# Four fused layers on one core: GpSimd makes both parts of W_hh, eight banks for columns, late products of 128 rows

## The chip, the core and the metric

The kernel runs on one core of one Trainium2 chip. Its engines are TensorE (PE, matrix products; PEld is its weight load), VectorE (DVE), ScalarE (ACT), GpSimd (POOL) and SyncE (SP, which here only issues transfers). Each runs its own list of instructions in order, and they wait for each other by semaphores. The metric is the device time of one execution in microseconds, as a median of several.

## What is computed

Four layers, each added to its input; `x` is 4 batches of 512 rows of 512 values in fp32.

```python
x = x + L0(fside, cond, x)      # a 0/1 mask of the 5120 largest entries of an outer product times softmax(x), per batch
x = x + L1(x, cond, W_emb, b_emb, g_norm, W_qkv, g_q, g_k, W_out)
    # xn = rms_norm(x) * g_norm * (1 + scale) + shift;  q, k, v = split(xn @ W_qkv), 16 heads of 32
    # q, k = rms_norm per head; o = softmax(q @ k.T / sqrt(32)) @ v;  returns o + o @ W_out
x = x + L2(cond, x, W_ih, W_hh, b_ih, b_hh)
    # a GRU over 512 steps: gi = x_t @ W_ih + b_ih, gh = h @ W_hh + b_hh, gates r, z, n, new h
x = x + L3(x, cond)             # each row sampled at 512 places given by cond, with linear interpolation
```

## The kernel before

It has one hand-written program for each engine (`pe_program`, `dve_program`, `act_program`, `pool_program`, `sp_program`); the order of the lines is the order of the work, and semaphores named in `SEMAPHORES` tie them. There are eight PSUM banks of 128 x 512 fp32, reached as `k.bank(i, ...)`.

First comes a search for the mask's threshold for all four batches. Then the attention of the batches runs one after another, `b` from 0 to 3. A batch has these stages:

- Columns (`pe_columns`, `act_columns`, `dve_columns`): PE transposes `x` (L1610) into banks 0 and 1, which DVE copies to `xT` (L1201), and multiplies it by a diagonal of the row norms (L1617) into banks 2 and 3, which ACT scales to `xnT` (L692). Four column groups `c`, two at a time, use the same four banks twice.
- Projection (`pe_project`, L1640) of four row tiles `t` to q, k and v, three outputs of 4 products each. For each tile ACT takes squares and copies (L704, L705), DVE sums, normalizes (L1230), and ACT and DVE split the heads to a high and a low fp16 part (L719, L1244), which PE transposes (`pe_turn_stack`, L1659) and ACT and DVE copy out (L728, L1252). POOL scales the keys between (`pool_keys`, L494). Beside this lie, for the next batch, the mask (`dve_mask_equal`, `dve_mask_prefix`, `dve_mask_quota`, `dve_mask_taken` on DVE, `pool_mask` on POOL) and the row powers (L675 on ACT); for the previous batch the output products (`pe_out_matmuls`, L1682), with POOL's L517 and DVE's L1261 that add to `xT`.
- The attention loop over 32 units, 8 for each of four head groups `g`. In a unit PE makes two score products (L1703), DVE their maxima (L1272), somebody negates them (L509 on POOL in batches 0 to 2, L1275 on DVE in batch 3), ACT takes exponentials (L743), PE transposes them (L1719), ACT and DVE copy the transposes (L788, L1351), and PE multiplies by the values (L1737). After each group DVE inverts the sums (L1359), POOL spreads them (L465), PE turns them (L1752, the divide), ACT copies (L750) and DVE multiplies (L1283, which counts `out_cols`).

In batch 3 there is no next batch. Instead DVE finds the scale of W_hh (`dve_hh_scale`), ACT writes the scaled fp16 high part `w_kept` (`act_high_weights`, L665), DVE the remainder in place (`dve_low_weights`, L1101), and POOL copies the high part behind it (`pool_keep_weights`, L485): chunks 0 and 1 after tile 1, chunks 2 and 3 after tile 2, as `WEIGHT_CHUNKS` says.

After the last batch's output products, PE makes the first gate products (L1814), and then the recurrence starts (`pe_gru`): 512 steps of 96 small products each (L1907). `SIDE` puts other products between the steps: gate products of later chunks (L1814) and the sampling of finished rows, 128 rows by 256 columns (L1841). The rows 384 to 447 are sampled from step 464 on by `pe_late_products` (L1854), with 64 rows in 4 products, two records each, at one product a step over 32 steps; rows 448 to 479 follow from step 496, the last 32 at the end.

Of the kernel before, what the change touches and what calls it, by code (L numbers as in the profile page):

```python
# [16 lines left out]
P = 128  # L17
B, S, D = 4, 512, 512
NT = S // P
# [53 lines left out]
prepared sums absmax hh_most hh_scale w_high w_low w_kept  # L73
# [299 lines left out]

R_BANK, Z_BANK, N_BANK, SIDE_BANK = (0, 3), (1, 4), (2, 5), (6, 7)


def sp_program(e, k):
# [43 lines left out]
def pool_program(e, k):  # L421
# [21 lines left out]
    for b in range(B):  # L443
# [27 lines left out]
WEIGHT_CHUNKS = ((), (0, 1), (2, 3), ())  # L471


# [8 lines left out]
def pool_keep_weights(e, k, c):  # L482
    s = k.sem
    e.wait_ge(s["w_low"], c + 1)
# [176 lines left out]
def act_high_weights(e, k, c):  # L661
    s = k.sem
    if c == 0:
        e.wait_ge(s["hh_scale"], 5)
    e.activation(k.w_kept[:, c], k.w_hh_raw[:, c], ACT.Copy, scale=k.hh[2][:]).then_inc(s["w_high"], 1)  # L665


# [16 lines left out]
def act_columns(e, k, b):  # L684
# [5 lines left out]
    for c in range(NC):  # L690
        e.wait_ge(s["normed_turned"], NC * b + c + 1)
        e.activation(k.xnT[:, c], k.bank(2 + c % 2, S), ACT.Identity, scale=k.col_scale[:, c, b:b + 1],  # L692
# [60 lines left out]
def act_attention(e, k, b, logit_scale):  # L753
    s = k.sem
    act_take_projected(e, k, b, 0)
    for t in range(1, NT):
# [6 lines left out]
        if b == B - 1:  # L763
            for c in WEIGHT_CHUNKS[t]:
                act_high_weights(e, k, c)
        elif t == 1:
            act_row_powers(e, k, b + 1)
        elif t == 2:
# [67 lines left out]
def act_take_late_rows(e, k, i, bank):  # L836
    s = k.sem
    b, part = divmod(i, ROW_GROUPS)
    rows = slice(0, LATE[1] - LATE[0])
# [258 lines left out]
def dve_low_weights(e, k, c):  # L1098
    s = k.sem
    e.wait_ge(s["w_high"], c + 1)  # L1100
    e.scalar_tensor_tensor(k.w16[:, c, 0].rearrange("p a n -> p (a n)"), k.w_hh_raw[:, c], k.hh[2][:], k.w_kept[:, c],  # L1101
                           ALU.mult, ALU.subtract).then_inc(s["w_low"], 1)


# [84 lines left out]
def dve_columns(e, k, b):  # L1189
# [9 lines left out]
    for c in range(NC):  # L1199
        e.wait_ge(s["x_turned"], NC * b + c + 1)  # L1200
        e.tensor_copy(k.xT[:, c, b], k.bank(c % 2, S)).then_inc(s["x_cols"], 1)  # L1201
# [98 lines left out]
def dve_attention(e, k, b):  # L1300
    s = k.sem
    if b + 1 < B:
        dve_mask_equal(e, k, b + 1)
        dve_mask_prefix(e, k, b + 1)
        dve_mask_quota(e, k, b + 1)
        dve_mask_taken(e, k, b + 1)
    else:
        dve_hh_scale(e, k)
    dve_take_projected(e, k, b, 0)
    for t in range(1, NT):  # L1310
# [3 lines left out]
        dve_stack(e, k, b, t - 1, 0)  # L1314
        dve_turn_stack(e, k, b, t - 1, 0)
        dve_stack(e, k, b, t - 1, 1)
        dve_take_projected(e, k, b, t)
        if b == B - 1:
            for c in WEIGHT_CHUNKS[t]:
                dve_low_weights(e, k, c)  # L1320
        elif t == 2:
# [276 lines left out]
def pe_columns(e, k, b):  # L1598
# [4 lines left out]
    for first in range(0, NC, 2):  # L1603
        for c in (first, first + 1):
            if c >= 2:
                e.wait_ge(s["x_cols"], NC * b + c - 1)
            elif b:
                e.wait_ge(s["exp"], 2 * len(UNITS) * b)
            for t in range(NT):
                made = e.transpose(k.bank(c % 2, S)[:, t * P:(t + 1) * P], k.x[:, b, t, c * P:(c + 1) * P], k.ident[:])  # L1610
            made.then_inc(s["x_turned"], 1)
        for c in (first, first + 1):
            e.wait_ge(s["diagonals"], NT * (b + 1))
            if c >= 2:
                e.wait_ge(s["x_normed"], NC * b + c - 1)
            for t in range(NT):
                made = e.matmul(k.bank(2 + c % 2, S)[:, t * P:(t + 1) * P], k.x[:, b, t, c * P:(c + 1) * P], k.diagonal[b][:, t],  # L1617
# [336 lines left out]
```

## Time and profile before

| | us |
|---|---|
| median of 3 runs | 2307.71 |
| lowest, highest | 2306.45, 2307.78 |
| profiled execution, its own time | 2310.08 |
| its span in the trace | 2308.4 |
| mean granted TensorE clock | 0.968 |
| PE busy | 2181.9 (95%) |
| DVE busy | 1558.8 (68%) |
| ACT busy | 1276.3 (55%) |
| POOL busy | 501.5 (22%) |

Busy time is an average over stages with different limits. The chain of work that ended last is followed backwards from the last instruction to what released each step, and tells where time could be won. Starts in the rows are microseconds from the start of the span; durations of PE are modelled at their ends, so that starts are the better measure of a pace.

### The profile page before, as it was taken

To read this page: it belongs to the slowest core of one execution; us is meant where nothing else is said; L and a number is where in the kernel's file an instruction comes from. 1 tells how busy PE (TensorE), PEld (TensorE's weight loads), DVE (VectorE), ACT (ScalarE), POOL (GpSimd) and SP (SyncE) were. 2 spreads that over 40 slices of the span, in tenths; PEclk is the share of its full clock that TensorE was granted. 3 is DMA by queue.
4 is the path that set the end of the run, shared out by engine and by line. 5 is a ranking of instruction groups with operands and counts; after the bars stand their busy time and mean duration, and the time that the engine had idled before them with its cause. 6 is when DMAs were issued, how large, how long until landed. Compare 5 with 4: busy or idle time off the path is not lost.

```text
span 2308.4 us, 132456 instructions
## 1 busy us (share of the span) xinstructions
PE 2181.9 (95%) x56333; PEld 1833.7 (79%) x56333; DVE 1558.8 (68%) x7118; ACT 1276.3 (55%) x5574; POOL 501.5 (22%) x2261
## 2 busy tenths in 40 slices
PE   5768999999989999999999999999999999999998
PEld 3654555645545799999999999999999999999887
DVE  7986867768678366666676666666666667666665
ACT  6755947758558344566444444544445444444443
POOL 2001121021110222233222222222222222222222
PEclk8568999999999999999999999999999999999999
DMA  5000000010010000000000000000000000000000
GB/s 202 3 2 1 1 1 1 2 55 1 1 55 1 21 5 5 5 5 5 5 5 10 5 10 5 10 10 5 10 9 5 9 5 10 10 5 14 12 9 16
DMA packets 8728, 31.63 MB, mean 14 GB/s; under 512 B 1028, under 2 KB 1352, under 8 KB 7880
## 3 DMA queue, kind: packets, MB, share of 16 engines
q1 hardware_dynamic: 7712, 23.07, 2.7%
q8 instruction: 444, 7.27, 1.3%
q14 instruction: 148, 1.21, 0.2%
q10 hardware_dynamic: 424, 0.07, 0.0%
HBM read 18.94 MB, written 4.19 MB: 10 GB/s over the span
## 4 chain that ended last, share of the span: by engine, by line
PE 84%; DVE 10%; ACT 3%; issue 2%; DMA 1%; POOL 0%; SPq 0%; DVEq 0%; POOLq 0%; ACTq 0%
PE psum L1907 52%; PE psum L1814 9%; PE psum L1640 5%; PE psum L1719 4%; PE psum L1737 3%; PE psum L1703 2%; PE psum L1682 2%; PE psum L1841 2%; DVE region_cols L1095 2%; DVE region_cols L1079 2%; DVE top L1272 1%; PE psum L1659 1%; DMA region_cols<-in_L_cond_W_emb_dram 1%; PE psum L1854 1%; PE psum L1752 1%
## 5 line engine op out<-in xcount | busy, mean ns | idle before, releaser
L1907 PE MATMUL psum<-parts0A,region_w_hh 128*128 128x40 f16 x12288 | 431.4, 182 | 3.4 <-DVE parts0A L1496 2.3
L1907 PE MATMUL psum<-parts1A,region_w_hh 128*128 128x40 f16 x12288 | 428.7, 181 | 2.9 <-DVE parts1A L1496 2.6
L1907 PE MATMUL psum<-parts0B,region_w_hh 128*128 128x40 f16 x12288 | 427.7, 181 | 0.4 <-issue 0.2
L1907 PE MATMUL psum<-parts1B,region_w_hh 128*128 128x40 f16 x12288 | 426.4, 181 | 0.6 <-issue 0.5
L1907 PEld LDWEIGHTS psum<-parts0A,region_w_hh 128*128 128x128 f16 x12288 | 381.0, 96 | 44.6 <-DVE parts0A L1496 11.5
L1907 PEld LDWEIGHTS psum<-parts1A,region_w_hh 128*128 128x128 f16 x12288 | 377.6, 96 | 44.9 <-DVE parts1A L1496 13.2
L908 ACT ACTIVATE mixA<-rzA 128x8 f32<-128x8 f32 x512 | 111.3, 217 | 541.9 <-DVE rzA L1451 541.9
L1907 PEld LDWEIGHTS psum<-parts0B,region_w_hh 128*128 128x128 f16 x12288 | 363.1, 96 | 1.6 <-issue 0.2
L1907 PEld LDWEIGHTS psum<-parts1B,region_w_hh 128*128 128x128 f16 x12288 | 361.4, 96 | 2.1 <-issue 0.8
L551 POOL TENSOR_SCALAR lineA<-lineA 128x8 f32<-128x8 f32 x511 | 121.7, 238 | 853.8 <-DVE lineA L1487 853.8
L1451 DVE TENSOR_REDUCE rzA<-psum 128x8 f32<-128x32 f32 x512 | 98.1, 192 | 255.6 <-PE psum L1907 254.3
L1814 PE MATMUL psum<-region_cols,region_w_a 128*128 128x256 f32 (+1 forms) x864 | 252.5, 389 | 0.9 <-DVE region_cols L1261 0.9
L743 ACT ACTIVATE region_rows<-psum,neg_top 128x512 f32<-128x512 f32 x256 | 173.9, 686 | 34.5 <-POOL neg_top L509 23.2
L551 POOL TENSOR_SCALAR lineB<-lineB 128x8 f32<-128x8 f32 x511 | 125.3, 245 | 287.4 <-DVE lineB L1487 287.4
L1272 DVE TENSOR_REDUCE top<-psum 128x2 f32<-128x1024 f32 x128 | 156.2, 1222 | 38.4 <-PE psum L1703 38.3
L915 ACT ACTIVATE giveB<-rzB 128x8 f32<-128x8 f32 x512 | 109.0, 213 | 131.4 <-DVE rzB L1458 131.0
L1640 PE MATMUL psum<-region_w_a,region_work 128*128 128x512 f32 x384 | 173.5, 605 | 3.5 <-ACT region_work L692 3.5
L1719 PEld LDWEIGHTS psum<-ident,region_rows 128*128 128x128 f32 x1024 | 118.5, 141 | 34.8 <-issue 18.7
L1466 DVE TENSOR_TENSOR_SCAN nlineA<-mixA,psum 128x32 f32<-128x32 f32 x512 | 113.0, 221 | 43.2 <-ACT mixA L908 0.7
L1719 PE MATMUL psum<-ident,region_rows 128*128 128x128 f32 x1024 | 136.2, 275 | 4.8 <-ACT region_work L788 4.1
L1640 PEld LDWEIGHTS psum<-region_w_a,region_work 128*128 128x128 f32 x384 | 72.2, 193 | 86.0 <-issue 81.7
L922 ACT ACTIVATE lineA<-nlineA 128x8 f32<-128x8 f32 x512 | 111.6, 218 | 47.4 <-DVE nlineA L1466 1.0
(245 smaller groups left out, 3709.1 us busy)
## 6 DMA issues: line engine op xcount, KB each, us to landing
region_rows<-in_x_dram SPq DMA_DIRECT2D x4, 1024.0 KB, 11.2
region_w_a<-in_L_cond_W_qkv_dram SPq DMA_DIRECT2D x1, 3072.0 KB, 23.1
region_w_hh<-in_L_cond_W_hh_dram SPq DMA_DIRECT2D x4, 768.0 KB, 6.4
region_w_a<-in_L_cond_W_ih_dram SPq DMA_DIRECT2D x1, 3072.0 KB, 10.3
out_dram<-region_w_b SPq DMA_DIRECT2D x12, 256.0 KB, 2.6
region_cond<-in_cond_dram SPq DMA_DIRECT2D x2, 1024.0 KB, 7.8
region_cols<-in_L_cond_W_emb_dram SPq DMA_DIRECT2D x1, 2048.0 KB, 19.7
region_w_out<-in_L_cond_W_out_dram SPq DMA_DIRECT2D x1, 1024.0 KB, 21.5
```

The lines of the kernel that those rows point to most:

```text
L551: e.tensor_scalar(k.line[half][:, :, :, 1], k.line[half][:, :, :, 2], -1.0, None, ALU.mult).then_inc(s[f"minus{h}"], 1)
L743: e.activation(k.probs[b][:, 2 * pair + i], k.bank(2 * pair + i, S), ACT.Exp, scale=logit_scale, bias=k.neg_top[:, col + i:col + i + 1], a ...
L908: e.activation(k.mix[half][:, :, :, 3], k.rz[half][:, 0], ACT.Sigmoid, scale=unscale).then_inc(s[f"rsig{h}"], 1)
L915: e.activation(k.give[half][:, :, :, 2], k.rz[half][:, 1], ACT.Sigmoid, scale=minus_unscale).then_inc(s[f"give{h}"], 1)
L922: e.activation(k.line[half][:, :, :, 0], k.nline[half][:, :, :, 3], ACT.Tanh, scale=unscale).then_inc(s[f"tanh{h}"], 1)
L1272: e.tensor_reduce(k.top[:, cols], k.psum[:, 2 * pair:2 * pair + 2], AX.X, ALU.max).then_inc(s["top"], 1)
L1451: e.tensor_reduce(k.rz[half][:, 0], k.slots(R_BANK[half])[:, 0], AX.X, ALU.add).then_inc(s[f"rsum{h}"], 1)
L1466: e.tensor_tensor_scan(k.nline[half][:].rearrange("p c b q -> p (c b q)"), k.mix[half][:].rearrange("p c b q -> p (c b q)"), k.bank(N_BANK ...
L1640: made = e.matmul(k.bank(bank, D), k.xnT[:, c, t * P:(t + 1) * P], k.w_qkv[:, c, i * D:(i + 1) * D], start=(c == 0), stop=(c == NC - 1))
L1719: made = e.transpose(k.bank(bank, NT, P)[:, kt], k.probs[b][:, slot, kt * P:(kt + 1) * P], k.ident[:])
L1814: made = e.matmul(k.bank(SIDE_BANK[number % 2], B * LENGTHS[q]), k.w_ih[:, c, block * P:(block + 1) * P], k.xT[:, c, :, STARTS[q]:STARTS[q ...
L1907: made = e.matmul(k.slots(bank)[:, :, ch, :, 0:2], k.w16[:, 2 * read + c, part, NC * "rzn".index(g) + 2 * half + ch], k.parts[now][read][: ...
```

## The change

Five edits. (1) `act_high_weights` and `dve_low_weights` are gone; a new `pool_split_weights` does all of it on POOL, one chunk before each wait for `inv_weight` in batch 3: a scaled copy to `w_kept`, a scaling of the raw chunk in place, their difference to the low part, the copy of the high part. (2) The columns stage has a bank for each of the eight products, with the order: two transposed groups, four normed groups, two transposed groups. The first projection waits for two of the four copies to `xT`, the second for all. (3) In batch 0 DVE's `dve_mask_quota` moves behind the taking of the first projection and `dve_mask_taken` behind the first stack. (4) The last batch's output products `m` = 0 and 1 first take three of four groups `c`, then the fourth, and then come `m` = 2 and 3. (5) The late products take 128 rows, 320 to 447, as weights; the 64 wanted ones are then in partitions 64 to 127, from where they are copied and written out.

```diff
+TURNED_BANK, NORMED_BANK = (0, 1, 4, 5), (2, 3, 6, 7)
@@ sp_program
-        e.dma_start(k.d_out[b, LATE[0]:LATE[1]], k.rows_out[0:LATE[1] - LATE[0], b]).then_inc(s[f"out{b}"], 16)
+        e.dma_start(k.d_out[b, LATE[0]:LATE[1]], k.rows_out[P - (LATE[1] - LATE[0]):, b]).then_inc(s[f"out{b}"], 16)
@@ pool_program
-            if t and b == B - 1:
-                for c in WEIGHT_CHUNKS[t]:
-                    pool_keep_weights(e, k, c)
         for g in range(NC):
+            if b == B - 1:
+                pool_split_weights(e, k, g)
@@
+def pool_split_weights(e, k, c):
+    s = k.sem
+    low = k.w16[:, c, 0].rearrange("p a n -> p (a n)")
+    if c == 0:
+        e.wait_ge(s["hh_scale"], 5)
+    e.tensor_scalar(k.w_kept[:, c], k.w_hh_raw[:, c], k.hh[2][:], None, ALU.mult).then_inc(s["w_high"], 1)
+    e.tensor_scalar(k.w_hh_raw[:, c], k.w_hh_raw[:, c], k.hh[2][:], None, ALU.mult).then_inc(s["w_scaled"], 1)
+    e.wait_ge(s["w_high"], c + 1)
+    e.wait_ge(s["w_scaled"], c + 1)
+    e.tensor_tensor(low, k.w_hh_raw[:, c], k.w_kept[:, c], ALU.subtract).then_inc(s["w_low"], 1)
     e.wait_ge(s["w_low"], c + 1)
     e.tensor_copy(k.w16[:, c, 1].rearrange("p a n -> p (a n)"), k.w_kept[:, c]).then_inc(s["w_kept"], 1)
@@ act_attention
-        if b == B - 1:
-            for c in WEIGHT_CHUNKS[t]:
-                act_high_weights(e, k, c)
@@ dve_attention
-        dve_mask_quota(e, k, b + 1)
-        dve_mask_taken(e, k, b + 1)
+        if b:
+            dve_mask_quota(e, k, b + 1)
+            dve_mask_taken(e, k, b + 1)
     dve_take_projected(e, k, b, 0)
+    if b == 0:
+        dve_mask_quota(e, k, b + 1)
     for t in range(1, NT):
         dve_norm_heads(e, k, b, t - 1)
         dve_stack(e, k, b, t - 1, 0)
+        if b == 0 and t == 1:
+            dve_mask_taken(e, k, b + 1)
...
-        if b == B - 1:
-            for c in WEIGHT_CHUNKS[t]:
-                dve_low_weights(e, k, c)
@@ pe_columns
+    for c in (0, 1):
+        pe_turn_rows(e, k, b, c)
+    for c in range(NC):
+        pe_norm_rows(e, k, b, c)
+    for c in (2, 3):
+        pe_turn_rows(e, k, b, c)
+def pe_turn_rows(e, k, b, c):
+    if b and c == 0:
+        e.wait_ge(s["exp"], 2 * len(UNITS) * b)
+    elif b and c >= 2:
+        e.wait_ge(s[("probs_act", "probs_dve")[c - 2]], len(UNITS) * b)
...
+def pe_norm_rows(e, k, b, c):
+    if b and c >= 2:
+        e.wait_ge(s[("out_cols", "inv_cols")[c - 2]], NC * b)
...
@@ pe_project
         if t == 0:
-            e.wait_ge(s["x_cols"], NC * (b + 1))
+            e.wait_ge(s["x_cols"], NC * b + 2)
         elif t == 1:
+            e.wait_ge(s["x_cols"], NC * (b + 1))
@@ pe_out_matmuls
-    e.wait_ge(s["out_cols"], NC * (b + 1))
+    e.wait_ge(s["out_cols"], NC * b + cs[-1] + 1)
@@ pe_attention
-        pe_out_matmuls(e, k, b, range(NC))
+        pe_out_matmuls(e, k, b, (0, 1), range(NC - 1))
+        pe_out_matmuls(e, k, b, (0, 1), range(NC - 1, NC))
+        pe_out_matmuls(e, k, b, (2, 3))
@@ pe_late_products
-        made = e.matmul(k.bank(SIDE_BANK[number % 2], HALF_ROW)[0:LATE[1] - LATE[0]], k.xT[:, c, b, LATE[0]:LATE[1]],
+        made = e.matmul(k.bank(SIDE_BANK[number % 2], HALF_ROW), k.xT[:, c, b, LATE[1] - P:LATE[1]],
```

## Rows read from the trace of the kernel before

**Rows 1.** The page: the chain that ended last, by engine.

```profile
PE 84%; DVE 10%; ACT 3%; issue 2%; DMA 1%; POOL 0%; SPq 0%; DVEq 0%; POOLq 0%; ACTq 0%
```

**Rows 2.** Stages of batches 2, 3: window, length, busy us (PE, PEld, DVE, ACT, POOL), clock.

```profile
455.77:515.83 60.06, 58.26 (x223) 28.34 (x224) 42.68 (x68) 28.50 (x46) 16.23 (x12) 1.00 0.14 53
604.27:671.52 67.25, 60.30 (x219) 29.36 (x220) 45.33 (x59) 31.48 (x41) 18.72 (x13) 0.95 0.13 47
```

**Rows 3.** Timeline of ACT, DVE and PE in batch 3: start, us, instruction, idle before.

```profile
631.15 3.02 ACT L665 ACTIVATE region_rows<-region_w_hh,hh_scale 128x1536 f16<-128x1536 f32 x2
...
632.75 3.55 DVE L1101 SCALAR_TENSOR_TENSOR region_w_hh<-region_w_hh,hh_scale,region_rows 128x1536 f16<-128x1536 f32 x2 [1.11 <-ACT region_rows L665]
...
641.84 1.89 PE L1659 MATMUL psum<-ident,region_work 128*128 128x128 f16 x16 [4.51 <-DVE region_work L1244]
...
659.15 1.07 PE L1659 MATMUL psum<-ident,region_work 128*128 128x128 f16 x16 [2.44 <-DVE region_work L1244]
```

**Rows 4.** POOL's groups by form: busy us, mean ns, idle before; then one timeline row.

```profile
L551 POOL TENSOR_SCALAR lineA<-lineA 128x8 f32<-128x8 f32 x511 | 121.7, 238 | 853.8 <-DVE lineA L1487 853.8
...
L558 POOL COPY region_work<-lineA 128x8 f32<-128x8 f32 x512 | 97.7, 191 | 1.6 <-DVE lineA L1487 1.6
...
L494 POOL TENSOR_TENSOR region_work<-region_work,gain 128x512 f32<-128x512 f32 x16 | 20.3, 1270 | 308.4 <-DVE region_work L1230 308.4
...
L465 POOL COPY region_cond<-inv_weight 128x512 f32<-128x512 f32 x16 | 9.8, 610 | 97.6 <-DVE inv_weight L1359 97.6
...
715.05 0.61 POOL L465 COPY region_cond<-inv_weight 128x512 f32<-128x512 f32 x1 [17.66 <-DVE inv_weight L1359]
```

**Rows 5.** DVE's L1244 beside POOL (timeline), and spreads of single durations in ns.

```profile
639.15 2.63 DVE L1244 TENSOR_TENSOR region_work<-region_work 128x512 f16<-128x512 f32 x2 [1.12 <-ACT region_work L719]
...
639.32 3.79 POOL L485 COPY region_w_hh<-region_rows 128x1536 f16<-128x1536 f16 x2
...
L1244 DVE TENSOR_TENSOR region_work<-region_work x32: 677/772/1943, 180.8 to 669.3; 128x512 f16<-128x512 f32 x32
...
L1275 DVE TENSOR_TENSOR neg_top<-top,minus_logit_scale x32: 160/161/163, 677.8 to 746.7; 128x2 f32<-128x2 f32 x32
```

**Rows 6.** Batch 3's loop, DVE's timeline.

```profile
710.10 0.16 DVE L1275 TENSOR_TENSOR neg_top<-top,minus_logit_scale 128x2 f32<-128x2 f32 x1
...
712.09 0.16 DVE L1275 TENSOR_TENSOR neg_top<-top,minus_logit_scale 128x2 f32<-128x2 f32 x1
...
714.90 1.16 DVE L1272 TENSOR_REDUCE top<-psum 128x2 f32<-128x1024 f32 x1
```

**Rows 7.** Columns of batch 3 on PE; DVE's `quota` in batch 1.

```profile
597.92 1.04 PE L1610 MATMUL psum<-ident,region_rows 128*128 128x128 f32 x8
...
598.79 1.95 PE L1617 MATMUL psum<-region_rows 128*128 128x128 f32 x16
...
604.27 20.87 PE L1640 MATMUL psum<-region_w_a,region_work 128*128 128x512 f32 x48 [0.87 <-ACT region_work L692]
...
318.24 0.16 DVE L1163 TENSOR_SCALAR quota<-psum 128x4 f32<-128x4 f32 x1 [2.18 <-PE psum L1595]
```

**Rows 8.** Batch 0, PE's first stack transposes.

```profile
183.27 1.06 PE L1659 MATMUL psum<-ident,region_work 128*128 128x128 f16 x16
```

**Rows 9.** The chain at the last divide and the output products.

```profile
752.80 1.10 PE psum L1752 x8
...
755.38 14.02 PE psum L1682 x32
```

**Rows 10.** PE's timeline: starts of steps with row products, then with late products.

```profile
2127.86 0.97 PE L1907 MATMUL psum<-parts0A,region_w_hh 128*128 128x40 f16 x32
...
2130.80 0.96 PE L1907 MATMUL psum<-parts1A,region_w_hh 128*128 128x40 f16 x32
...
2154.40 0.97 PE L1907 MATMUL psum<-parts1A,region_w_hh 128*128 128x40 f16 x32
...
2160.57 0.60 PE L1907 MATMUL psum<-parts1A,region_w_hh 128*128 128x40 f16 x17
```

More of the change, by code:

```diff
@@ L72 @@
 const vec emb_products emb_rows row_max weighted exp_rows diagonal keys_act keys_dve
-prepared sums absmax hh_most hh_scale w_high w_low w_kept
+prepared sums absmax hh_most hh_scale w_high w_scaled w_low w_kept
 mask_made mask_summed sum_copied counted ranked signed bound highs lows
@@ L658, in act_bound @@
     e.activation(k.bound[:, col], old, ACT.Identity, scale=2.0, bias=k.way[:, col]).then_inc(s["bound"], 1)
[L661 to L665, printed above, removed]
 def act_row_powers(e, k, b):
@@ L691, in act_columns @@
         e.wait_ge(s["normed_turned"], NC * b + c + 1)
-        e.activation(k.xnT[:, c], k.bank(2 + c % 2, S), ACT.Identity, scale=k.col_scale[:, c, b:b + 1],
+        e.activation(k.xnT[:, c], k.bank(NORMED_BANK[c], S), ACT.Identity, scale=k.col_scale[:, c, b:b + 1],
                      bias=k.col_shift[:, c, b:b + 1]).then_inc(s["x_normed"], 1)
@@ L762, in act_attention @@
         act_take_projected(e, k, b, t)
-        if b == B - 1:
-            for c in WEIGHT_CHUNKS[t]:
-                act_high_weights(e, k, c)
-        elif t == 1:
+        if b + 1 < B and t == 1:
             act_row_powers(e, k, b + 1)
-        elif t == 2:
+        elif b + 1 < B and t == 2:
             act_row_roots(e, k, b + 1)
@@ L838, in act_take_late_rows @@
     b, part = divmod(i, ROW_GROUPS)
-    rows = slice(0, LATE[1] - LATE[0])
+    rows = slice(P - (LATE[1] - LATE[0]), P)
     e.wait_ge(s["rows_sum"], TILE_ROWS + i + 1)
@@ L1095, in dve_mask @@
         e.tensor_scalar(mask, k.lows[:, b], 2.0 ** -(LOW_BITS - 1 - i), k.bound[:, col], ALU.mult, ALU.is_ge).then_inc(s["mask_made"], 1)
[L1098 to L1102, printed above, removed]
 def dve_mask_equal(e, k, b):
@@ L1200, in dve_columns @@
         e.wait_ge(s["x_turned"], NC * b + c + 1)
-        e.tensor_copy(k.xT[:, c, b], k.bank(c % 2, S)).then_inc(s["x_cols"], 1)
+        e.tensor_copy(k.xT[:, c, b], k.bank(TURNED_BANK[c], S)).then_inc(s["x_cols"], 1)
 def dve_take_projected(e, k, b, t):
@@ L1317, in dve_attention @@
         dve_take_projected(e, k, b, t)
-        if b == B - 1:
-            for c in WEIGHT_CHUNKS[t]:
-                dve_low_weights(e, k, c)
-        elif t == 2:
+        if b + 1 < B and t == 2:
             dve_row_scales(e, k, b + 1)
@@ L1602, in pe_columns @@
         e.wait_ge(s["bound"], B * (HIGH_BITS + LOW_BITS))
[L1603 to L1617, printed above, removed]
-                                start=True, stop=True)
-            made.then_inc(s["normed_turned"], 1)
+    for c in (0, 1):
[10 more added lines that the diff above has]
+        e.wait_ge(s[("probs_act", "probs_dve")[c - 2]], len(UNITS) * b)
+    for t in range(NT):
+        made = e.transpose(k.bank(TURNED_BANK[c], S)[:, t * P:(t + 1) * P], k.x[:, b, t, c * P:(c + 1) * P], k.ident[:])
+    made.then_inc(s["x_turned"], 1)
+def pe_norm_rows(e, k, b, c):
+    s = k.sem
+    if c == 0:
+        e.wait_ge(s["diagonals"], NT * (b + 1))
+    if b and c >= 2:
+        e.wait_ge(s[("out_cols", "inv_cols")[c - 2]], NC * b)
+    for t in range(NT):
+        made = e.matmul(k.bank(NORMED_BANK[c], S)[:, t * P:(t + 1) * P], k.x[:, b, t, c * P:(c + 1) * P], k.diagonal[b][:, t],
+                        start=True, stop=True)
+    made.then_inc(s["normed_turned"], 1)
 def pe_project(e, k, b, t, outputs):
```

2 lines of the change are left out of this document (removed).

## The prediction

> **What bounds the kernel now.** I read the page first. The chain that ended last is 84% TensorE (PE) [rows 1]. So PE's own work or what PE waits for is worth time; VectorE (DVE), ScalarE (ACT) and GpSimd (POOL) count only where PE stands. Next I cut the span by the chain into the search, four attention batches, the output products of the last one (755.38 to 769.40) [rows 9] and the recurrence. The stage table then compares like with like: from the first projection to the third output product, batch 2 takes 60.06 us with PE busy 58.26, batch 3 67.25 with PE busy 60.30 at a mean granted clock of 0.95 of its upper level, 2.4 GHz [rows 2]. Batch 3 has two holes, 4.51 and 2.44 us, both ended by DVE's L1244; before each, ACT's L665 and DVE's L1101 work on W_hh [rows 3]. The lower clock, seen in this window and not in batch 2's, comes with the first hole.
>
> **W_hh leaves ACT and DVE.** Four L665 and four L1101 go. Two pairs of 3.02 and 3.55 us [rows 3] overlap only in part, so up to 5 us of delay lies ahead of each L1244. Without them PE is next late at its own pace: batch 2 shows 58.3 us of work for the same stage, and batch 3 has no L675 on ACT. That would give 67.25 - 58.3 = 9.0 us.
>
> **W_hh goes to POOL.** A chunk is now a scaled copy to fp16, a scaling in place, a subtraction and the known copy L485, two of which take 3.79 us [rows 5], each over 1536 columns. The trace has no long POOL TENSOR_SCALAR. With 8 columns it takes 238 ns where a copy takes 191 [rows 4], so I take the copy's 1.9 us; the lower end is 1.5, from L465 (610 ns for 512 fp32), the upper the price of a two-input operation. That one is L494 or L517 at 1.27 us for 512, less some 0.15 of fixed cost three times over: 3.5 us. A chunk is 1.9 + 1.9 + 3.5 + 1.9 = 9.2 us, at most 12.4. POOL stands idle 17.66 us before each spread L465 [rows 4], so the spread, and PE's divide behind it, are not late. Nor is the start of the recurrence, which waits for `w_low` and `w_kept`: chunk 3 starts near 734 and ends before 750.
>
> **What that cover hides badly.** DVE and POOL hold each other up. At 639.15 two L1244, some 1.3 us by the least single time (677 ns, the ends overlapping), took 2.63: its second, due at about 639.8, ran only when POOL's copy (639.32 + 1.90) had ended [rows 5]. One L1244 took 1943 ns against a median of 772 [rows 5]. I read it as: a DVE operation with both inputs in SBUF waits for the whole POOL operation under way, then goes ahead of the next. In batch 3's loop that is L1275, the negated maximum, once per unit of 1.98 us; behind it on DVE is queued the copy L1351 that PE's next transposes wait for, and ACT's exponentials (L743) wait for L1275 itself. L1275 never met POOL (160 to 163 ns), so the bounds are nothing and full blocking; I take full blocking, because L1244 has the same kind of operation and of inputs. The page "SBUF — State Buffer" of the Trainium skill, section Who interferes with whom, says the same of a DVE instruction with two SBUF inputs beside a GpSimd instruction that reads SBUF, and calls one with at most one SBUF input free outside the two-port modes. By that rule the loop loses the 8.7 us worked out next; if it does not reach an operation on two columns, the loop loses nothing and 8.7 us come back.
>
> In the loop DVE runs reduce, L1275, copy; none of the rows names an idle time before them, 710.10 to 712.09 being one unit [rows 6]. A chunk starts at about 715.7, after the spread (715.05 + 0.61) [rows 4]. The next L1275 comes at 716.06, the end of the reduce begun at 714.90, and waits to 717.6: 1.5 us. Another comes 1.9 us after it, when the in-place scaling is just over: 0. The next meets the subtraction: 3.5 - 1.9 = 1.6. The last copy costs 0 again. That is 3.1 us a chunk, 2.9 with what slack PE has, and chunks 1 to 3 cost 3 x 2.9 = 8.7. Chunk 0 starts at the end of L494 of the last tile, just when the last four L1244 want to run (the last of one kind starts at 669.3) [rows 5]. Each lets one POOL operation pass; the fourth ends behind the subtraction, some 5 us after PE could use it. Of the 9.0 us, 9.0 - 5.1 = 3.9 are left. Net of all W_hh edits: 3.9 - 8.7 = -4.8, a loss.
>
> **Eight banks for columns, and the first batch's order.** Now PE runs transposes and normed products in two rounds and ACT finishes after the last, from 597.92 to 604.27: 6.35 us [rows 7]. Of this PE stands the last 0.87 for ACT's L692. Two groups of transposes take 0.87 by the starts (597.92 to 598.79). In the new order PE does just these while ACT finishes, so the stage is 6.35 - 0.87 = 5.5, a gain of 0.9. DVE gets its last two columns about 1.6 us later, so its mask or scale work starts later. In batches 1 and 2 it stood 2.18 us before `quota` (row at 318.24) [rows 7], which covers it but for some 0.3: gain 0.6 each. In batch 3 DVE is done before PE's first stack transposes: 0.9. In batch 0 the same step gives 1.1, PE's slow first products at the start of the stage unchanged. There the delay would eat DVE's margin, but `quota` and `taken` move behind the first projection's taking and the first stack, and a wait such as batch 1's is filled; PE reaches its first stack transposes at 183.27 with no idle either way [rows 8]. POOL's mask and ACT's L675 behind `taken` keep their place. New waits on banks 4 to 7 are for things done long before. Sum 1.1 + 0.6 + 0.6 + 0.9 = 3.2.
>
> **Output products of the last batch.** PE stands from the end of the divide, 752.80 + 1.10 = 753.90, to 755.38 for ACT's L750 and DVE's L1283 [rows 9]. Six of the 16 products (14.02 x 6/16 = 5.3 us) now fill this. The end moves by 1.5. The last addition still comes behind m = 3, and POOL's four L517 (at about 1.3 each, as L494) stay ahead of the additions.
>
> **Late products.** Two of the 32 late steps take 2160.57 - 2154.40 = 6.17 us, 3.085 each; a step with L1841, the same moving shape but 128 x 128 weights, takes 2.94 (2127.86 to 2130.80) [rows 10]. So the bigger load hides, and the 64-column form does not. 32 x 0.145 = 4.6. Lower end 0, if the reason is not the shape. The eight copies out of partitions 64 to 127 cost what they did.
>
> **Sum.** -4.8 + 3.2 + 1.5 + 4.6 = 4.5 us. The profiled execution took 2310.08 with a span of 2308.4 and would take 2305.6; its execution lies 2.4 above the median 2307.71, so the median comes to 2303.2. I write 2303.
>
> **Rivals.** (1) L1275 is not held up, or only for what is left of a short piece. For it: no small DVE operation of the recurrence is ever long beside POOL's. Against: L1244. Then 8.7 come back, and perhaps 3 before the loop: 2303 - 8.7 to 11.7 = 2291 to 2294. (2) POOL's scaling costs more than the copy: the slower side. Two more L1275 per chunk meet longer operations. With p us for a scaling, the delay is (p - 0.35) + (p - 1.9) + 1.6. At p = 3.5 that is 6.3 a chunk, 18.3 for three after slack, and 3 more before the loop: 2303 + 9.6 + 3 = 2316. It cancels the gain of 4.5 us at about p = 2.5 (8 us for each us of p) and decides above that. (3) The 64-row form is not what lengthens the late steps: 2303 + 4.6 = 2307.8. (4) The W_hh edit does what it is for and chunk 0 hurts less, because the fourth L1244 gets in before the subtraction: 2299.
>
> **How the numbers follow.** Forecast 0.40 (with the L1244 variant (4) 0.08 more), rival 1 0.22, rival 2 0.20, rival 3 0.10. Range: the forecast's own is 2298 to 2308. To the low side it takes in the upper half of rival 1, to the high side rival 2 up to p of about 3.3: 2291 to 2314. A measurement here can tell about 0.2% from no change, 4.6 us: under 2303.1 is faster, over 2312.3 slower. The forecast sits on that line and is split: 0.20 faster, 0.20 same. With (4) and rival 1: faster 0.50. Rival 2 is slower 0.15 and same 0.05; rival 3 same 0.10: same 0.35, slower 0.15.
>
> **What would show it.** After: batch 3's stage with PE busy near 58.3 and the clock at 1.00, and a hole only before the last stack transposes; L1275 with a maximum of 1.5 us or more, some six long ones in the loop, and the idle of POOL before the spreads shorter by a chunk and the groups of batch 3 about 3 us longer each; POOL's four kinds at 1.9, 1.9, 3.5, 1.9; columns in 5.5; PE not idle after the last divide; late steps at 2.94. If L1275 stays at 161 ns, rival 1 holds; if a POOL TENSOR_SCALAR takes over 2.5 us, rival 2.

## The result, and the profile after

The changed kernel takes 2314.23 us in the median of 7 runs (2313.90 to 2315.85), the kernel before 2307.71 (2304.02 to 2308.12). The ratio is 1.0033, with a 95% interval of 1.0022 to 1.0044. So it is slower, by 6.5 us in the medians, where 4.5 us of gain were forecast. The two profiled executions are only 4.0 us apart, with spans of 2312.4 and 2308.4 us: the one of before lay 2.4 us above its median. All steps below are set against these two spans. The changed kernel's execution lay at its median, so the spans show 2.4 us less of the loss than the medians do.

PE's share of the chain that ended last has gone from 84% [rows 1] to 80%, and DVE's from 10 to 13%. First the page of the changed kernel, the chain by engine:

```profile
PE 80%; DVE 13%; ACT 3%; issue 3%; DMA 1%; POOL 0%; SPq 0%; DVEq 0%; POOLq 0%; ACTq 0%
```

The starts on PE, stage by stage, show where time came from and where it went (us from the start of the span; an ordinary table, read off the timelines):

| point | before | after | shift |
|---|---|---|---|
| batch 3, first projection | 604.27 | 600.07 | -4.20 |
| batch 3, first row maximum (DVE) | 676.54 | 666.68 | -9.86 |
| last divide starts | 752.74 | 765.77 | +13.03 |
| gate products start | 770.25 | 781.53 | +11.28 |
| recurrence starts | 782.06 | 793.35 | +11.29 |
| end of the span | 2308.4 | 2312.4 | +4.0 |

The columns and the stage in front of the loop gain 9.86 us, more than the 7.1 forecast. The loop of batch 3 loses 22.9 where 8.7 were forecast. Everything behind it gains. The loop alone made the sign. The first two rows are to be read with care: the trace of before is a late one. `late_alone` and `out_alone` below, which change nothing ahead of the last projection, reach it at 601.70 and 601.65 instead of 604.27.

Two stretches of batch 3 in the changed kernel, the stage up to the first maximum and the loop: window, length, busy us of PE, PEld, DVE, ACT and POOL (with counts), granted clock, DMA.

```profile
600.07:666.68 66.61, 63.55 (x256) 31.81 (x256) 42.77 (x62) 27.70 (x39) 22.50 (x12) 0.97 0.13 48
666.68:766.86 100.18, 76.36 (x611) 45.67 (x610) 87.15 (x104) 63.76 (x163) 43.30 (x18) 0.95 0.00 1
```

The same two stretches of the kernel before (its stage is longer here than in [rows 2], which ended sooner):

```profile
604.27:676.54 72.27, 64.56 (x255) 32.21 (x256) 48.24 (x64) 33.53 (x43) 18.72 (x13) 0.95 0.12 44
676.54:753.90 77.36, 70.24 (x610) 43.08 (x608) 65.43 (x104) 63.60 (x163) 2.45 (x4) 1.00 0.01 1
```

The loop is 22.8 us longer, DVE is "busy" for 21.7 us more with the same 104 instructions, and ACT's busy time is unchanged. A busy time that grows with an unchanged count suggests that instructions wait while they count as busy. The line that takes longer is the negated maximum, L1275 before [rows 5] and L1263 now; its durations in ns (least, median, most):

```profile
L1263 DVE TENSOR_TENSOR neg_top<-top,minus_logit_scale x32: 160/162/2844, 667.9 to 759.7; 128x2 f32<-128x2 f32 x32
```

Its neighbours in one group of the loop, from the timeline of all engines (start, us). It answers [rows 6]:

```profile
688.16 4.16 POOL L484 TENSOR_SCALAR region_rows<-region_w_hh,hh_scale 128x1536 f16<-128x1536 f32 x1
688.62 2.84 DVE L1263 TENSOR_TENSOR neg_top<-top,minus_logit_scale 128x2 f32<-128x2 f32 x1
...
691.50 0.69 ACT L741 ACTIVATE region_rows<-psum,neg_top 128x512 f32<-128x512 f32 x1 [2.78 <-DVE neg_top L1263]
...
692.30 4.16 POOL L485 TENSOR_SCALAR region_w_hh<-region_w_hh,hh_scale 128x1536 f32<-128x1536 f32 x1
...
693.23 2.37 DVE L1263 TENSOR_TENSOR neg_top<-top,minus_logit_scale 128x2 f32<-128x2 f32 x1
...
696.61 3.10 POOL L488 TENSOR_TENSOR region_w_hh<-region_w_hh,region_rows 128x1536 f16<-128x1536 f32 x1
...
697.36 2.37 DVE L1263 TENSOR_TENSOR neg_top<-top,minus_logit_scale 128x2 f32<-128x2 f32 x1
...
699.77 1.46 POOL L490 COPY region_w_hh<-region_rows 128x1536 f16<-128x1536 f16 x1
```

The reader is to see three long L1263 per chunk, one for each POOL operation except the short copy. They wait 2.68 + 2.21 + 2.21 = 7.1 us beyond their own 0.16 (in the chunks of this and the next two groups; a tenth L1263, of 1.12 us, stands at the loop's start behind the last copy of chunk 0), and ACT's exponentials stand behind the first one for 2.78 us. The group of the next chunk takes 25.26 us, from the divide at 701.60 to the one at 726.86, where the kernel before took 18.27 (703.83 to 722.10). The difference is 6.99. The group after it takes 26.55, at a mean granted clock of 0.87. The two windows, with the same columns as above:

```profile
701.60:726.86 25.26, 17.47 (x156) 10.61 (x153) 23.25 (x28) 16.19 (x42) 13.46 (x5) 1.00 0.01 2
726.86:753.41 26.55, 20.68 (x156) 12.65 (x153) 23.24 (x28) 16.30 (x42) 13.46 (x5) 0.87 0.00 1
```

PE does the same 156 instructions in both, and takes 3.2 us more for them in the second.

POOL's groups by form between 650 and 765 us (busy us, mean ns), the answer to [rows 4] and the price that had no row in the trace of before:

```profile
L484 POOL TENSOR_SCALAR region_rows<-region_w_hh,hh_scale 128x1536 f16<-128x1536 f32 x4 | 17.6, 4404 | 0.0
L485 POOL TENSOR_SCALAR region_w_hh<-region_w_hh,hh_scale 128x1536 f32<-128x1536 f32 x4 | 16.8, 4196 | 0.0
L488 POOL TENSOR_TENSOR region_w_hh<-region_w_hh,region_rows 128x1536 f16<-128x1536 f32 x4 | 12.4, 3099 | 0.6
L490 POOL COPY region_w_hh<-region_rows 128x1536 f16<-128x1536 f16 x4 | 5.9, 1464 | 0.3
```

### The profile page after: what moved, and what is told of

Read it like the earlier page. It is cut to its first block, busy times and chain, and to the rows that moved or that the text cites. A ratio compares the mean times of both kernels' runs of the same rounds, so it can differ in the third digit from the quotient of the medians.

```text
span 2312.4 us, 132462 instructions
## 1 busy us (share of the span) xinstructions
PE 2178.6 (94%) x56333; PEld 1837.6 (79%) x56333; DVE 1572.7 (68%) x7114; ACT 1272.1 (55%) x5570; POOL 549.8 (24%) x2273
## 4 chain that ended last, share of the span: by engine, by line
PE 80%; DVE 13%; ACT 3%; issue 3%; DMA 1%; POOL 0%; SPq 0%; DVEq 0%; POOLq 0%; ACTq 0%
PE psum L1912 52%; PE psum L1819 9%; PE psum L1643 4%; PE psum L1722 3%; PE psum L1740 2%; PE psum L1846 2%; PE psum L1706 2%; DVE top L1260 2%; PE psum L1685 2%; DVE region_cols L1090 2%; DVE region_cols L1074 2%; PE psum L1662 1%; DVE region_work L1341 1%; DMA region_cols<-in_L_cond_W_emb_dram 1%; PE psum L1755 1%
## 5 line engine op out<-in xcount | busy, mean ns | idle before, releaser
L1722 PE MATMUL psum<-ident,region_rows 128*128 128x128 f32 x1024 | 139.7, 278 | 21.4 <-DVE region_work L1341 17.3
## 6 DMA issues: line engine op xcount, KB each, us to landing
region_w_a<-in_L_cond_W_qkv_dram SPq DMA_DIRECT2D x1, 3072.0 KB, 22.9
```

Of the source, the lines that this page charges most:

```text
L1722: made = e.transpose(k.bank(bank, NT, P)[:, kt], k.probs[b][:, slot, kt * P:(kt + 1) * P], k.ident[:])
```

## The experiments

Two theories went in. **Theory A:** each long POOL operation holds up L1263, which has two inputs in SBUF, until it is over, and the scalings are dearer than the forecast had them. **Rivals:** the loss comes from another part of the change (columns, output products, late products); POOL's work holds DVE up in some other way, for instance by its total and not by the length of one instruction; or every DVE operation is held, so that no other form would help. Ratios are to the kernel before on the same chip; times in us that stand beside them are the ratio times 2307.7. The recurrence wanders by some microseconds from run to run in stretches that no edit touches (steps 192 to 448 took 753 to 762 us in the kernels below), so a stage's own length in the trace is given where it decides.

### Without the W_hh part

The changed kernel, with ACT and DVE making W_hh as before:

```
-            if b == B - 1:
-                pool_split_weights(e, k, g)
...
+        if b == B - 1:
+            for c in WEIGHT_CHUNKS[t]:
+                act_high_weights(e, k, c)
...
+        if b == B - 1:
+            for c in WEIGHT_CHUNKS[t]:
+                dve_low_weights(e, k, c)
```

> The changed kernel with the W_hh edit taken back (ACT and DVE split it as before), all other edits kept. Theory (the loop's negated maxima wait behind POOL's long scalings, and this is the whole loss): by the two traces the loop lost 22.9 us and the stage before it gained 5.7, so 17 us come back: 2297, with batch 3's groups again 18.3 us apart and L1263 at 162 ns. Rival (part of the loss is in the new order of banks or in the recurrence): less than 12 us come back.

Ratio 0.9958 (0.9944 to 0.9972), 17.3 us under the changed kernel. The groups of the loop are back at 18.27 us, and the last divide starts at 751.61.

### The W_hh part alone

The kernel before with `pool_split_weights` in the loop of its last batch and without L665 and L1101.

> The kernel before with the W_hh edit alone. Theory: the same 17 us on top of 2307.7, so 2325, three negated maxima of 2.84, 2.37 and 2.37 us in each of three groups. Rival (the edits work on each other): clearly more or less than 17.

Ratio 1.0068 (1.0052 to 1.0085), +15.7 us. Its groups took 26.15 and 27.07 us. With the run above this lays the loss on W_hh: the rival of another part is gone. Its stage in front of the loop takes 64.95 us (72.27 before), so all of the loss is in the loop.

### The other three parts alone

Each is put into the kernel before by itself. The late products:

```
-        made = e.matmul(k.bank(SIDE_BANK[number % 2], HALF_ROW)[0:LATE[1] - LATE[0]], k.xT[:, c, b, LATE[0]:LATE[1]],
+        made = e.matmul(k.bank(SIDE_BANK[number % 2], HALF_ROW), k.xT[:, c, b, LATE[1] - P:LATE[1]],
```

> The kernel before with one part of the change: the late rows' products use 128 columns of weights and write 128 rows, of which the last 64 are taken. If the 64-column form is what makes a late step 3.085 us instead of 2.94, the time falls by 32 x 0.145 = 4.6 us against before, all of it between steps 464 and 496. If it is something else that sits in those steps (the 0.45 us every second product, the side bank's wait), it is the time of before within 1 us.

Ratio 0.9989 (0.9979 to 0.9999), -2.5 us. The part's own stretch is plainer. These are ACT's first activation of steps 464 and 496 in the kernel before:

```profile
2152.74 0.22 ACT L908 ACTIVATE mixA<-rzA 128x8 f32<-128x8 f32 x1 [0.85 <-DVE rzA L1451]
...
2251.52 0.22 ACT L908 ACTIVATE mixA<-rzA 128x8 f32<-128x8 f32 x1 [0.96 <-DVE rzA L1451]
```

and in the changed kernel:

```profile
2162.21 0.22 ACT L903 ACTIVATE mixA<-rzA 128x8 f32<-128x8 f32 x1 [0.85 <-DVE rzA L1441]
...
2257.18 0.22 ACT L903 ACTIVATE mixA<-rzA 128x8 f32<-128x8 f32 x1 [0.78 <-DVE rzA L1441]
```

98.78 us before, 94.97 after. Late products alone gave 94.53; the three other kernels without this edit gave 98.78 to 99.10, and all with it 94.2 to 95.7. So the 64-row form was the cause. It is worth 3.8 us in the changed kernel and 4.2 alone, where 4.6 were forecast. The edit changes the width of the weights and the partitions of the result together; which of the two counts was not told apart.

The columns' stage, with the first batch's order:

> The kernel before with the columns' stage in eight banks and with the batch 0 order of DVE's mask, nothing else. By the stage's lengths in the changed kernel (10.02 to 8.75 us in batch 0, 0.87 us less in each of the other three) and the 0.42 us that batches 1 and 2 lose in between, it gains 1.27 + 2.61 - 0.84 = 3.0 us against before. If the gain of a shorter stage is given back further on, as part of it was there, it is within 1 us of before.

Ratio 0.9985 (0.9976 to 0.9994), -3.5 us. The stage itself is plain: from the last divide of a batch to the next first projection every kernel without the edit takes 7.35 us and every one with it 6.47 or 6.48, three times each. Up to the last batch's projection this run is 3.68 us ahead of the trace of before (600.59 against 604.27), but that trace is a late one. The four kernels without the edit arrive at 601.65 to 604.27, 602.95 in the mean, the ten with it at 598.70 to 601.88, 599.82 in the mean. The difference is 3.1 us.

At the first maximum only 1.98 of the 3.68 us are left. From the second hole of [rows 3] to the last stack transposes, in the kernel before, with the columns alone, and with the late products alone (window, length, PE busy, clock, DMA):

```profile
659.15:673.17 14.02, 13.27 (x72) 1.00 0.50 205
```

```profile
655.47:671.19 15.72, 14.96 (x72) 0.89 0.43 181
```

```profile
656.57:672.28 15.71, 14.95 (x72) 0.89 0.43 180
```

The same 72 instructions take 1.7 us longer at a mean clock of 0.89, so a part of the stretch ran at the lower of the two levels, 1.2 GHz. It lies right behind a hole of PE of 2.63 us, which is 2.44 us in [rows 3]. But this is no price of the new columns. The late products alone, with before's code in this stretch, show it too, behind a hole of 2.78 us, and so do the output products alone (15.71 us, behind 2.80). From the first projection to the first maximum these two take 73.95 us each and the columns alone 73.97, where the trace of before has 72.27. The odd one is before's: there the clock stayed up.

The output products:

```
-        pe_out_matmuls(e, k, b, range(NC))
+        pe_out_matmuls(e, k, b, (0, 1), range(NC - 1))
+        pe_out_matmuls(e, k, b, (0, 1), range(NC - 1, NC))
+        pe_out_matmuls(e, k, b, (2, 3))
```

> The kernel before with the last batch's output products ordered as in the change (three groups of two banks before the last divide's result is awaited), nothing else. The distance from the last divide to the gate products was 16.35 us before and 14.60 after: if that shortening carries to the end, the time falls by 1.5 to 1.75 us. If the first output products then stand in the way of the last divide or the adds, it is within 0.5 us of before. The step lengths of the recurrence wander by more than that from run to run, so the stage's own length in the trace decides, not the median alone.

Ratio 0.9991 (0.9982 to 0.9999), -2.1 us. From the last divide the chain goes on without a pause (start, us), where [rows 9] has 1.48 us between them:

```profile
751.87 1.09 PE psum L1752 x8
752.96 13.75 PE psum L1682 x32
```

The four parts alone add up to 15.7 - 2.5 - 3.5 - 2.1 = +7.6 us, and the whole change measured 1.0033, +7.6. That both are 7.6 is luck: the intervals of the four alone are 2 to 4 us wide to each side. No sign of the parts working on each other is seen, and one of a few us could hide.

### POOL's instructions in pieces

The cut keeps all of POOL's work and its order and takes away only the length of one instruction. Each operation of a chunk is cut into n parts of 1536 / n columns:

```
+    parts = [slice(768 * i, 768 * (i + 1)) for i in range(2)]
+    for q in parts:
+        made = e.tensor_scalar(k.w_kept[:, c, q], k.w_hh_raw[:, c, q], k.hh[2][:], None, ALU.mult).then_inc(s["w_high"], 1)
...
+    for i, q in enumerate(parts):
...
+        e.tensor_tensor(low[:, q], k.w_hh_raw[:, c, q], k.w_kept[:, c, q], ALU.subtract).then_inc(s["w_low"], 1)
```

Four pieces of 384:

> The changed kernel with each of POOL's 16 operations cut into four of 384 columns; POOL's work is the same or a little more. Theory (a DVE operation waits for the POOL operation under way, not for the chunk): a piece of scaling takes 1.1 to 1.2 us, each negated maximum waits at most that and about 0.45 on average, some 7 of them a chunk, 3.2 us a chunk in place of 7.1, and the four L1232 before the loop wait about 2 us less: 2314 - 11.7 - 2 = 2300 to 2303. Rival (POOL's total time or its use of memory slows DVE): no gain, 2314 or above.

Ratio 0.9919 (0.9901 to 0.9936), -18.7 us, some 11 us under what was expected, and the fastest of all kernels here, 2291.94 us in the median. Its two stretches of batch 3:

```profile
599.41:661.89 62.48, 61.72 (x256) 30.96 (x256) 40.04 (x62) 27.68 (x39) 18.40 (x15) 1.00 0.13 51
661.89:740.00 78.11, 70.73 (x611) 43.19 (x610) 66.90 (x104) 63.80 (x163) 57.30 (x63) 1.00 0.01 1
```

In the loop POOL is busy 57.3 us instead of 43.3, and the loop is 22 us shorter. So it is not POOL's total that hurts. In a group, with POOL's pieces from 683.55 to 699.3, L1271 (the same line here) is near its own time:

```profile
683.55 4.91 POOL L486 TENSOR_SCALAR region_rows<-region_w_hh,hh_scale 128x384 f16<-128x384 f32 x4
```

```profile
684.00 0.16 DVE L1271 TENSOR_TENSOR neg_top<-top,minus_logit_scale 128x2 f32<-128x2 f32 x1
...
689.93 0.32 DVE L1271 TENSOR_TENSOR neg_top<-top,minus_logit_scale 128x2 f32<-128x2 f32 x1
```

The groups take 18.27 us, as without POOL's work. The sign was forecast, the size was not: 3.2 us of waits a chunk were expected, and in each of the groups of chunks 1 to 3 only one L1271 waits, for 0.16 us. The model in the expectation, a wait to the end of the piece under way, is not what these scalings show.

Two pieces of 768:

> The changed kernel with each of POOL's instructions of a chunk cut into two of 768 columns (four pieces of 384 gave groups of 18.3 us again and ratio 0.992). If VectorE's small product waits for the end of the POOL instruction under way, a piece of 2.1 to 2.4 us holds it for up to 1.5 us, the longest of the negated maxima are 1.2 to 1.7 us, the groups take 19 to 21 us, and the time is 2 to 8 us under before. If only long instructions of POOL hold it, or if it gets in whenever POOL is between instructions and the loop has 0.8 us to spare, it is as with four pieces: negated maxima under 0.9 us, groups of 18.3 us, 18 to 20 us under before.

Ratio 0.9939 (0.9924 to 0.9954), -14.1 us: between the two expectations. The waits are 0.25 to 0.36 us, five in a group, 1.4 us in sum, and the groups take 19.30 us, 1.03 more than without POOL. Expected were longest L1271 of 1.2 to 1.7 us, from waits to the end of a piece. Two pieces of a scaling and the L1271 beside them:

```profile
684.49 4.38 POOL L486 TENSOR_SCALAR region_rows<-region_w_hh,hh_scale 128x768 f16<-128x768 f32 x2
```

```profile
684.95 0.45 DVE L1271 TENSOR_TENSOR neg_top<-top,minus_logit_scale 128x2 f32<-128x2 f32 x1
687.17 0.41 DVE L1271 TENSOR_TENSOR neg_top<-top,minus_logit_scale 128x2 f32<-128x2 f32 x1
```

Each L1271 is over 0.91 us after the start of a piece that lasts 2.20. In the changed kernel it was over 3.30 us after the start of a scaling of 4.16. So theory A's "until it is over" does not hold for the scalings; it holds for the subtraction and the copy, as the last section shows.

Eight pieces of 192:

> The changed kernel with each of POOL's instructions of a chunk cut into eight of 192 columns, where four of 384 gave ratio 0.9919 and groups of 18.27 us, the same as with no POOL work in them. If the loop has nothing left to give, groups stay at 18.3, the stacks in front of the loop lose at most 0.3 us more of their waits, and the time is that of four pieces within 2 us (17 to 21 us under before). If a fixed cost of about 0.3 us per piece lengthens a chunk (16 us with four pieces, some 21 us with eight) past the 18.27 us of a group, the last chunk ends later and delays the recurrence: 3 us or more above four pieces.

Ratio 0.9930 (0.9918 to 0.9943), -16.2 us. The mechanism of the second expectation is there. A piece of a scaling took 0.76 us where one twice as wide took 1.25, so a chunk with its spread grew to 19.9 us, more than a group's 18.27. The chain shows the price, POOL's pieces and then its spread ahead of the last divide:

```profile
739.93 2.09 POOL region_w_hh L498 x7
742.01 0.57 POOL region_cond L465
742.63 2.08 PE psum L1763 x8
```

The recurrence starts at 771.81, 5.3 us after that of four pieces (766.48). In the ratios the two are only 2.5 us apart, less than the 3 us expected and within what these can tell.

### What a scaling costs

The scalings as products of two tensors:

```
-    e.tensor_scalar(k.w_kept[:, c], k.w_hh_raw[:, c], k.hh[2][:], None, ALU.mult).then_inc(s["w_high"], 1)
+    e.tensor_tensor(k.w_kept[:, c], k.w_hh_raw[:, c], k.hh[2][:].broadcast_to([P, 1536]), ALU.mult).then_inc(s["w_high"], 1)
```

> The changed kernel, with POOL's two scalings of a chunk written as a product of two tensors, the second one the factor broadcast over the 1536 columns. If the form of the instruction made the scalings take 4.16 us where a product of two tensors takes 3.1, the chunk is 2.1 us shorter, VectorE is held 2 x 1.06 us less in each of three chunks and about as much in front of the loop, and the time falls by about 8 us against the changed kernel, to 1 or 2 below the kernel before. If both forms cost the same, it is the time of the changed kernel, 6 above before. If a broadcast operand is dearer still, it is slower than that by three times the difference.

```profile
693.09 2.75 POOL L484 TENSOR_TENSOR region_rows<-region_w_hh,hh_scale 128x1536 f16<-128x1536 f32 x1
```

A scaling falls from 4.16 to 2.75 us, and the groups from 25.3 to 22.4: three waits of 2.12, 0.78 and 1.33 us, 4.23 in sum, for 4.11 us of a group. But the ratio is 1.0017 (1.0008 to 1.0027), -3.7 against the changed kernel where 8 were expected. The miss lies in front of the loop. There the stacks' two-input operations (L1232) met the dense two-input POOL work worse than they met the scalings:

```profile
654.78 3.93 DVE L1232 TENSOR_TENSOR region_work<-region_work 128x512 f16<-128x512 f32 x2 [1.12 <-ACT region_work L717]
658.63 6.72 DVE L1232 TENSOR_TENSOR region_rows<-region_work,region_rows 128x512 f16<-128x512 f32 x2
```

The same four took 1.38 + 4.26 us in the changed kernel, and that stage is 5.4 us longer than there (72.05 against 66.61). Some of it is the clock, 0.93 in the mean of that stage against 0.97.

The factor as a number in the instruction (65536 for these inputs) instead of a value per partition:

> The changed kernel with the factor of POOL's two scalings of a chunk written into the instruction as the number 65536 instead of read from a tile with one value per partition (it is the value that the tile holds for these inputs; another input would need another number). If the reading of the per-partition value makes 4.16 us of the scaling, where a product of two tensors took 2.75, a scaling now takes 1.9 to 2.9 us and the groups of the loop take 20 to 23 us instead of 25.3: 6 to 15 us under the changed kernel. If it is the instruction's kind that takes 4.16 us, whatever the factor is read from, scaling, groups and time are those of the changed kernel.

```profile
689.67 4.08 POOL L484 TENSOR_SCALAR region_rows<-region_w_hh 128x1536 f16<-128x1536 f32 x1
```

4.08 instead of 4.16, groups of 25.08 us, ratio 1.0038 (1.0025 to 1.0050). So it is not the reading of the factor that makes POOL's TENSOR_SCALAR slow.

### Which operations of DVE wait

The negated maximum as a scaling by a per-partition value, one SBUF tensor in, over three columns:

```
-        e.tensor_tensor(k.neg_top[:, cols], k.top[:, cols], k.minus_logit_scale[:].broadcast_to([P, 2]), ALU.mult).then_inc(s["neg_top"], 1)
+        e.tensor_scalar(k.neg_last[:, n], k.top_last[:, n], k.minus_logit_scale[:], None, ALU.mult).then_inc(s["neg_top"], 1)
```

> The changed kernel with batch 3's negated maximum made by a TENSOR_SCALAR with a pointer for the factor over three columns (two wanted, one of zeros), in tiles of its own, in place of a TENSOR_TENSOR of two SBUF tensors. Theory (two SBUF inputs are what makes DVE wait; one input over an odd number of columns does not): the negated maximum stays below 0.2 us beside POOL's scalings and the loop's 21 us come back, while what chunk 0 costs before the loop stays: 2293. Rival (every DVE operation on SBUF waits for POOL): 2314.

Ratio 1.0026 (1.0013 to 1.0038): nothing gained. The expectation, that a DVE operation with one SBUF input over an odd number of columns goes past POOL, fell. It waits, and longer:

```profile
688.50 3.72 DVE L1269 TENSOR_SCALAR region_rows<-region_rows,minus_logit_scale 128x3 f32<-128x3 f32 x1
693.10 3.26 DVE L1269 TENSOR_SCALAR region_rows<-region_rows,minus_logit_scale 128x3 f32<-128x3 f32 x1
```

```profile
688.04 4.16 POOL L486 TENSOR_SCALAR region_rows<-region_w_hh,hh_scale 128x1536 f16<-128x1536 f32 x1
692.17 4.16 POOL L487 TENSOR_SCALAR region_w_hh<-region_w_hh,hh_scale 128x1536 f32<-128x1536 f32 x1
```

The same line as a reduction over one value per column, with the sign turned. It leaves out the factor of the logits, so that the shift in the exponentials is another one:

```
+        e.tensor_reduce(k.neg_top[:, cols], k.top[:, cols].unsqueeze(2), AX.X, ALU.max, negate=True).then_inc(s["neg_top"], 1)
```

> The changed kernel with the negated maximum of the last batch made by VectorE's reducing instruction over one value per column with its sign turned, so that it reads one SBUF tensor and no scalar. It leaves out the factor of the logits in that shift, so the shift is larger than the largest scaled logit; the number and size of the instructions are the same. The run with three columns and a per-partition factor (3.72 us at most) still waited for POOL. If what waits is an instruction that takes a second read path (two SBUF inputs, or a copy or scaling that can run two elements at a time), a reducing instruction doesn't: the negated maxima take 0.15 to 0.3 us beside POOL's scalings, the groups of the loop 18.3 us, and the time is some 21 us under the changed kernel, ratio 0.992 to 0.995. If every VectorE instruction from SBUF to SBUF waits for the POOL instruction under way, it has some nine of 2.2 us or more, groups of 25 us, and the changed kernel's time, ratio 1.003.

Ratio 0.9926 (0.9906 to 0.9946), -17.1 us. POOL's operations are those of the changed kernel, and DVE no longer sees them:

```profile
687.24 4.16 POOL L484 TENSOR_SCALAR region_rows<-region_w_hh,hh_scale 128x1536 f16<-128x1536 f32 x1
691.38 4.16 POOL L485 TENSOR_SCALAR region_w_hh<-region_w_hh,hh_scale 128x1536 f32<-128x1536 f32 x1
```

```profile
L1263 DVE TENSOR_REDUCE neg_top<-top x32: 154/155/157, 667.5 to 736.5; 128x2 f32<-128x2 f32 x32
```

Its groups take 18.27 us. One instruction of 0.16 us in another form is worth 24.7 us against the changed kernel (1.0033 - 0.9926). That settles the rival in which every DVE operation is held: the form of the operation decides. The page "SBUF — State Buffer" of the Trainium skill, section Who interferes with whom, says just this of a reduction, and it lets a scaling contend where it can run in a mode that takes both of DVE's ports. The page "Vector Engine (DVE) Microarchitecture Reference" of the Trainium skill, section Performance modes — why throughput varies by op and dtype, has the conditions of that mode; by them an odd count fulfils them when source and destination have the same, which is so for the three columns. By that the run with three columns was no test of the one-input rule, and both runs agree with the pages.

## Why the prediction was wrong

**The step that failed** is a term that was mis-sized: "so I take the copy's 1.9 us". It came from a copy and from an operation on 8 columns, [rows 4] and [rows 5], and its upper end was the price of a two-input operation, 3.5. The scaling took 4.16 us in the loop and up to 5.13 in front of it, beyond the upper bound. By the formula of rival 2, (p - 0.35) + (p - 1.9) + 1.6, p = 4.16 gives 7.7 us a chunk. Measured were 7.1 us of waiting and 6.99 us on a group. So the mechanism forecast was right, L1275 waiting behind POOL's long operations, and the time went the way of rival 2, whose sign (a POOL TENSOR_SCALAR over 2.5 us) came. What was wrong was the weight, 0.20 for a price on which no row of before bore.

Two agreements are partly luck. The 7.7 us of the formula are 3.81 + 2.26 + 1.6, the 7.1 measured are 2.68 + 2.21 + 2.21: the first term was too dear, since the wait ends 0.86 us before the scaling does, and the third too cheap. And 2314 is near rival 2's 2316 only because 2316 was reckoned with p = 3.5. At 8 us for each us of p, p = 4.16 gives about 2321. The loop did what this says; in front of it the change did some 7 us better.

**Point by point.**

- W_hh leaves ACT and DVE: 9.0 forecast. The stage takes 72.27 us before and 62.48 with four pieces, in which chunk 0 costs little: 9.8. In the two traces with before's stage and the lower clock (73.95) it would be 11.5.
- Chunk 0 in front of the loop: 5.1 forecast, 66.61 - 62.48 = 4.1 measured. With the W_hh part alone, where the clock stayed up, the stage takes 64.95, so that chunk 0 costs about 2.5 and the rest may be the clock (0.97 in the mean of the stage). The hole before the last stack transposes is there as foretold, but DVE's last L1232 is over at 660.25 and the subtraction begins at 664.43, the case of rival 4.
- The chunk: 9.2 us forecast, 12.4 at most; 4.16 + 4.16 + 3.10 + 1.46 = 12.9 measured. The subtraction (3.5) and the copy (1.9) were too dear. It still fits into the 17.66 us in which POOL stands [rows 4], as forecast.
- Waits in the loop: 2.9 a chunk forecast, 7.0 measured. Six long L1275 were foretold, two for each chunk; there are nine, three each, because the second scaling now also meets one. With 1.3 us more in the second group, where the clock fell, this makes 22.3 of the 22.8 us measured, instead of 8.7. That is 14.1 us too little, more than the whole miss of 8.5 us (-4.5 forecast, +4.0 in the spans; 11.0 us by the medians).
- Columns: the stage of batch 3 forecast at 5.5 us, measured 5.48 by the same starts (594.59 to 600.07). Its chain in the changed kernel (start, us) runs on PE without a stop, where [rows 7] has the 0.87 us behind ACT:

```profile
594.76 0.87 PE psum L1608 x8
595.63 3.57 PE psum L1619 x32
599.20 0.87 PE psum L1608 x8
600.08 1.12 PE psum L1643 x2
```

- Of the forecast 3.2 us, 3.1 arrive at the last projection in the mean of the traces. The 4.20 us of the first table hold 1 us of the late start of before's trace as well.
- Output products: 1.5 forecast, 16.35 - 14.60 = 1.75 measured.
- Late products: 4.6 forecast, 3.8 measured (4.2 with this edit alone). The last 16 late steps take 2.92 us each, as the model step did; the first 16 take 3.01, for a reason not looked into.
- The sum by what was measured up to the recurrence: -9.86 + 22.9 - 1.75 = +11.3. Then -3.8 for the late steps. The remaining 3.5 us by which the changed kernel's recurrence was shorter lie in stretches that no edit touches; that part of the +4.0 stays unexplained, and is as large as what such stretches wander from run to run.

## What to carry to other kernels

Before an engine is given work "in its idle time", ask which instructions of the neighbour it can hold up, and for how long one of its instructions lasts: here one chunk of 12.9 us, in 18 us of idle time, cost 7 us, and the same work in pieces of 1.25 us nothing. Cut such work into pieces (halves left 1.4 us of waits in a group, quarters 0.2), but not into so many that their fixed cost fills the idle time; or give the small operation on the critical path a form that does not wait. A price that the trace does not hold is to be bounded by more than the rows at hand: a kind of instruction seen only on 8 columns says nothing about 1536.

## What the runs showed of the hardware

- POOL's TENSOR_SCALAR over 1536 fp32 columns takes 4.16 us, 2.7 ns a column, more than a product of two tensors (2.75 us, and 3.10 for the subtraction) and nearly three times an fp16 copy (1.46). With 768 columns it takes 2.20, with 384 1.25, with 192 0.76.
- How long the two-input negated maximum (L1263, L1271) waits depends on POOL's operation. Beside a subtraction or a copy it ends with it, at every width: 699.73 and 699.71 us over 1536 columns, 695.04 and 695.02 over 768, 668.36 and 668.35 over 384, 695.97 and 695.96 over 192.
- Beside a scaling it is over earlier: 3.30 us after the start of one of 4.16, 0.91 of 2.20, 0.60 of 1.25, 0.44 of 0.76. So halving the scaling of 1536 columns took away more than two thirds of the hold, and that is why pieces help so much. Why the last step is so large was not tested.
- DVE's scaling form of three columns waited to the end of both kinds: 692.22 us for POOL's scaling that ended at 692.20, 699.60 for a subtraction that ended at 699.58.
- POOL pays too: the first scaling of chunk 0, started while DVE's stack operations ran, took 5.13 us.
- Holes of PE of 2.63 to 2.83 us in front of the same transposes were followed by a stretch at the lower clock in four traces (the columns, late and output products alone, and the kernel without the W_hh part); the hole of 2.44 us in before was not.
